# Moving the token load from SyncE's DMA queue to ScalarE's in a graph-attention, linear-attention and expert layer

## What is computed

```python
q = x @ wq.T + bq
k = x @ wk.T + bk
v = x @ wv.T + bv
q2 = (q @ wiq.T + biq).reshape(N, H, D).transpose(1, 0, 2)
...
scores = jnp.einsum('hnd,hmd->hnm', q2, k2) * scale + mask[None]
...
h = _masked_grouped_mm(routed_in.astype(jnp.bfloat16), w_up.astype(jnp.bfloat16), onehot)
h = jnp.square(jax.nn.relu(h.astype(jnp.bfloat16)))
routed_out = _masked_grouped_mm(h.astype(jnp.bfloat16), w_down.astype(jnp.bfloat16), onehot)
...
hs = jnp.square(jax.nn.relu(xf @ shared_w_up.T))
shared_out = hs @ shared_w_down.T
```

## Time and profile before

| | us |
|---|---|
| median of 3 runs | 362.57 (362.42 to 362.68) |
| the profiled execution, its own time | 362.45 |
| its span, first to last instruction | 360.6 |
| PE busy | 310.0 |
| DVE busy | 113.7 |
| ACT busy | 60.6 |
| POOL busy | 57.1 |

### The profile page before, as it was taken

How to read it: one execution, slowest core, us unless ns; L and a number is a source line. 1 busy time by engine, 2 the same in 40 slices (tenths; PEclk the granted TensorE clock), 3 DMA queues, 4 the chain that set the end, 5 groups by cost and what they waited for, 6 DMA issues and landing times.

```text
span 360.6 us, 3651 instructions
## 1 busy us (share of the span) xinstructions
PE 310.0 (86%) x1390; PEld 161.6 (45%) x1390; DVE 113.7 (32%) x258; ACT 60.6 (17%) x123; POOL 57.1 (16%) x106
## 2 busy tenths in 40 slices
PE   5999998999999999999599979899899866375374
PEld 4344434343443343433255556638566644144142
DVE  7609406410170658303822022301233321021011
ACT  1410000010003010300020042300342431031031
POOL 0511111121211212312400012300132300000000
PEclk9999999999999999999969999999999998588588
DMA  8999999999999999999999999999999999999994
GB/s 292 368 298 378 343 329 368 349 388 384 315 310 420 348 276 423 344 345 366 276 334 257 284 434 292 213 212 228 209 209 228 209 207 226 209 211 225 214 207 107
DMA packets 15593, 104.92 MB, mean 291 GB/s; under 512 B 1760, under 2 KB 2200, under 8 KB 6620
## 3 DMA queue, kind: packets, MB, share of 16 engines
q0 software_dynamic: 14112, 98.57, 96.1%
q1 hardware_dynamic: 1168, 5.98, 4.3%
q10 hardware_dynamic: 300, 0.19, 0.2%
HBM read 150.48 MB, written 0.39 MB: 418 GB/s over the span
## 4 chain that ended last, share of the span: by engine, by line
PE 76%; DMA 14%; another core or an unknown queue 3%; DVE 3%; ACT 2%; issue 1%
PE bank L825 43%; DMA stage<-in_expert_down 14%; PE bank L1006 8%; PE bank L992 7%; PE bank L967 6%; PE bank L1037 5%; PE bank L794 1%; PE bank L955 1%; PE bank L833 1%; PE bank L946 1%; ACT xn L422 1%; PE bank L809 1%; DVE xn L748 1%; PE bank L1018 0%
## 5 line engine op out<-in xcount | busy, mean ns | idle before, releaser
L825 PE MATMUL bank<-ring,xnt 128*96 128x512 f32 x224 | 99.5, 601 | 0.7 <-ACT xnt L358 0.6
L825 PEld LDWEIGHTS bank<-ring,xnt 128*96 128x96 f32 x224 | 36.4, 165 | 58.4 <-issue 57.4
L992 PE MATMUL bank<-stage,late 128*96 128x512 bf16 (+1 forms) x192 | 45.5, 391 | 18.4 <-DMA stage<-in_expert_up 17.9
L1006 PE MATMUL bank<-stage,hbuf 128*96 128x128 bf16 (+2 forms) x352 | 44.2, 285 | 11.5 <-DMA stage<-in_expert_down 7.9
L1006 PEld LDWEIGHTS bank<-stage,hbuf 128*96 128x96 bf16 x352 | 32.1, 127 | 23.6 <-issue 13.3
L825 PE MATMUL bank<-ring,stage 128*96 128x512 f32 x96 | 42.1, 593 | 0.0
L992 PEld LDWEIGHTS bank<-stage,late 128*96 128x96 bf16 x192 | 24.2, 133 | 34.1 <-issue 23.2
L422 ACT ACTIVATE xn<-bank 96x512 bf16<-96x512 f32 (+2 forms) x26 | 14.6, 561 | 87.0 <-PE bank L992 70.3
L748 DVE TENSOR_TENSOR xn<-xn 96x512 bf16<-96x512 bf16 (+1 forms) x24 | 9.6, 399 | 57.7 <-ACT xn L422 57.7
L763 DVE TENSOR_TENSOR acc<-acc_t,acc 96x128 f32<-96x128 bf16 (+2 forms) x32 | 13.5, 421 | 43.1 <-ACT acc_t L447 42.5
L825 PEld LDWEIGHTS bank<-ring,stage 128*96 128x96 f32 x96 | 15.3, 163 | 22.9 <-issue 22.9
(11 more groups left out here) (160 smaller groups left out, 207.4 us busy)
## 6 DMA issues: line engine op xcount, KB each, us to landing
stage<-in_expert_down POOLq DMA_DIRECT2D x8, 1408.0 KB, 28.9
stage<-in_expert_up POOLq DMA_DIRECT2D x5, 2048.0 KB, 32.5
stage<-in_expert_up POOLq DMA_DIRECT2D x6, 1024.0 KB, 12.8
stage<-in_expert_up POOLq DMA_DIRECT2D x8, 768.0 KB, 25.6
stage<-in_expert_down POOLq DMA_DIRECT2D x8, 704.0 KB, 31.8
stage<-in_expert_down POOLq DMA_DIRECT2D x16, 352.0 KB, 33.5
ring<-in_shared_down POOLq DMA_DIRECT2D x2, 2816.0 KB, 13.7
ring<-in_shared_up POOLq DMA_DIRECT2D x5, 1024.0 KB, 14.8
```

The lines of the kernel that those rows point to most:

```text
L825: ins = mm(bank[BANKS[m] + h][0:N, :], tiles(src)[:, k, :], w[:, kk, :], start=(k == 0), stop=(k == KT - 1))
L992: ins = mm(bank[4 + j][0:N, 0:c1 - c0], tiles(xe)[:, k, :], w[:, k, :], start=(k == 0), stop=(k == KT - 1))
L1006: ins = mm(bank[j][0:N, 0:c1 - c0], tiles(e_h)[:, t, :], w[:, t, :], start=(t == 0), stop=(t == TT - 1))
```

## The change

The load of `x` is taken from the head of SP's list and put at the head of ACT's. The first instruction of SP is now the load of the first piece of `wq`. Semaphores, buffers and all computing instructions stay as they are.

```diff
         @block.sync
         def _(sp):
-            sp.dma_start(xs[0:N, 0:D], x).then_inc(x_landed, 16)
 
             for piece in range(SLOTS):
                 load_piece(sp, piece)
...
         @block.scalar
         def _(act):
 
+            act.dma_start(xs[0:N, 0:D], x).then_inc(x_landed, 16)
             act.dma_start(edge_r, edge_rows).then_inc(rows_landed, 16)
             act.dma_start(cols[:], columns).then_inc(cols_landed, 16)
             act.dma_start(bias_v_b[0:1, :], bias_v).then_inc(bias_v_landed, 16)
```

## The result

| | before | after |
|---|---|---|
| median of the runs, us | 362.49 (362.29 to 362.68, 6 runs) | 366.01 (365.63 to 366.98, 6 runs) |
| ratio | | 1.0096, 95% interval 1.0086 to 1.0106 |
| the profiled execution, us | 362.45 | 366.08 |
| its span, us | 360.6 | 364.2 |

The change makes the kernel 3.5 us slower. The forecast was 362.2 us with a range of 361.7 to 364.5, so both the likeliest case and the range were wrong. Rival 1, in which the edge rows starve behind x, names the right mechanism. In its expensive version it gave 365.9 us.

The account below looks back on a forecast made before the run. It took the never-pausing DMA stream as the bound; the time changes by the larger of -h and d - s (1.2 - 2.65). With -0.4 taken, 362.45 became 362.05, plus 0.12 for the median: 362.2 us, range 361.7 to 364.5.

Parts of the forecast that it names:

- the likeliest case: Stream starts 0.2 to 0.7 us earlier and the backlog absorbs PE's delay: 362.2 us, chance 0.37.
- Rival 1: At the start, edge rows land late behind x beside `wq`: 364.3 us, 365.9 in the expensive version; chance 0.33.
- The principle: Whole kernel: a delay on PE costs nothing as long as the DMA stream does not run dry.
- d: Lateness of PE's first projection, through later edge rows: 0.2 to 1.7 us, taken as 1.2.
- s: Lateness the stream's backlog swallows, from the shortest refill distance at 62.61 us: about 2.65 us (1.45 to 4.1).
- h: At the kernel's start, how much earlier the DMA stream starts: 0.6 us, between 0 and 0.8.
- strict alternation: At the start, the two queues take turns packet by packet: edge rows land at 6.4 us, d = 2.2.
- Turns of about 0.6 us: Pace of ACT's queue beside `wq`, read from `columns`: 0.6 to 0.67 us a packet, passing about two of SP's.
- 5.25 less 2.3 less 0.3: Sum for s at 62.61 us: shortest distance, less a new transfer's start, less counting the landing: 2.65 us.

Follow-up runs that it names:

- the edge rows behind `wq` 0: Kernel before, with the edge rows moved from ACT's queue to SP's behind the first piece of `wq`, x still first on SP: 365.53 us (1.0083).

## Why the prediction was wrong

- **The principle held.** The stream sets the end; PE reaches it through POOL's refills only; the price is d - s. The prediction named the case in which the principle itself would be wrong (a later end with no window that shows an idle DMA). It did not come, and the kernels with repeated key matmuls confirm the path from PE to the stream.
- **h, forecast 0.6 us earlier, came out 0.7 us later.** The step that failed is the reading of the gap in the earlier trace rows as two requests worked off one after the other, ACT's first. It was SP's data that came first, in both kernels at 1.76 us: ten rows of x before, 14 rows of `wq` after. The 41 KB that the prediction took for the edge rows and one more block were those ten rows, the edge rows started at 2.53, and ten engines were busy in what looked like a gap. There was no head start to win. What the stream lost instead lies mostly in the time when x and `wq` alternate and each packet takes longer (0.39 us for 0.31, 0.20 for 0.16); up to 9 us that is 0.55 us by the estimate above. ACT's issue of 0.64 us at the start, on which the reading leaned, belongs to the edge rows' transfer and not to the first place: it takes 0.65 us at its new place, and x's issue in front of it takes 0.41.
- **d, forecast 1.2 (0.2 to 1.7), came out at 3.82.** That followed in large part from h. Without its head start x ran beside `wq` almost wholly. Rival 1's lower bound for d, by strict alternation, was 2.2 us and its upper 4.0 to 4.7; the first held from below and 3.82 lies just short of the second. Turns of about 0.6 us were right for x (7 turns from 2.78 to the landing at 7.13 are 0.62 each), but by luck. The list of packets shows strict alternation, 52 rows of x to 60 of `wq` from 3 to 5 us, and a turn is one stretched packet of each, 0.20 + 0.39 us, not one of ACT's and two of SP's. In the kernel before, the packets of `columns` start only at 5.21 and end at 7.65, one to one with `wq` too (98 to 92 from 5 to 7 us), which is 0.3 us a turn; the 0.6 read off spread them over 2 us and more in which they had not begun. So for what followed x the turns were too long: the edge rows landed at most 0.9 us after x (line 497 starts at 7.99), and `columns` at 10.65.
- **A term was missing:** 0.74 us from PE's slow first matmuls, which makes the lateness at the refills 4.56. No row of before could have given its size, but the weight loads at line 825 in the trace of before showed that the stretch is there.
- **s, forecast 2.65 (1.45 to 4.1), is about 1.** The step that failed is "5.25 less 2.3 less 0.3". It took 2.6 us as the distance under which the stream runs dry. The 2.3 us for a start were about right: the refill into an empty stream has 16 packets under way 2.1 us after its issue. (The 0.3 us for a landing stood on no row; in the kernel before, x's last packet ends at 3.81 and x has landed at 4.56.) What was wrong is to count from the landing before. Some DMA engines run out ahead of it, after the change from 68.0 us on for a landing at 70.5, and from 22.0 on for one at 23.3, and the packets with which they start again are slow. So most refills already lose at distances of 3 to 4 us. By that, 5.25 less 4 leaves 1.25 for s.
- **The sum with the measured terms:** d at the refills 4.56, s 0.8 to 1.4 by the other kernels whose refills are more than 4 us late, and 3.2 to 3.8 comes out; measured 3.5. How much of it is the stream's own late start of 0.7 us is known from one comparison only: with the edge rows behind `wq` 0 the stream starts in time, and the backlog swallowed 1.4 us instead of 1.0, so it is some 0.4. Part of this closeness may be luck, for the unexplained steps in the landings lie in the same sum.
- **The chances.** Rival 1 had 0.33 where the forecast had 0.37, and its price leaned on the mean s. With the bounds that the text itself named, d = 4.7 and s = 1.45, it stood at 365.9. The range stopped at 364.5 and left that out.

## What to carry to other kernels

Where one stream of transfers sets the end, the first small transfers decide when the compute engines begin to hand buffers back, so they belong in front of the bulk, on the same queue or with the bulk issued behind them; on a second queue beside the bulk a 384 KB transfer took 6.4 to 8.8 us, for 3.8 in front of it and 3.6 alone on that second queue. To price a late consumer, list for each refill the distance to the landing before it. Here two in three transfers with a distance under 4 us landed late, so the reserve is the shortest distance less 4, not less the time that a transfer needs to start. And before a short window is called a gap, look for packets that started ahead of it.

## What the runs showed of the hardware

- A 1 MB transfer issued by POOL into an empty stream landed after 5.0 us, where back to back the landings are 2.45 us apart. Its first data started 1.3 us after the issue.
- The first packets at the start take 0.67 to 1.18 us (8 KB) and 0.70 to 0.96 us (4 KB), for 0.31 and 0.16 us in the full stream. The first data of the program started at 1.66 to 1.82 us in all 16 kernels, about 1.0 us after the first issue, whichever transfer and queue was first.
- With x and `wq` on two queues their packets, one for each row, start about one for one (52 to 60 from 3 to 5 us), and both kinds slow down: a row of `wq` takes 0.39 us for 0.31, one of x 0.20 for 0.16.
- The issue of the edge rows' transfer (24 rows of 1 KB) takes 0.62 to 0.65 us wherever it stands in ACT's queue and 0.42 to 0.45 on SP's; that of x (96 rows) takes 0.32 to 0.41.
- The first float32 matmuls of a projection run at half rate for 3.2 to 6.0 us, also differently in kernels with the same PE instructions. The column of the granted clock reads 1.00 there because the trace has no record before the clock is full.
- The landings have steps of 0.4 to 1.7 us that no short distance goes with, also where 10 to 27 us are queued. Their cause is open.
